# Attention loop with both heads in 64-row tiles of TensorE, walked in half-pair periods

## Chip, cores and metric

One core of a Trainium2 chip runs the whole program, and the metric is the time of the core on the device, in microseconds (us). TensorE has two granted clock levels, 1.2 and 2.4 GHz; the profile writes them as 0.5 and 1.0 of full speed.

## Reference, cut to what matters

Two layers run one after the other on x of 2 x 512 tokens x 128 channels. The first is a FiLM-conditioned transformer block with one head. The second has attention with 16 heads of 64 channels and then an expert-choice mixture with 8 experts. The change is nearly all in the second layer's attention:

```python
qkv = (h @ Wqkv.T).reshape(b, n, 3, H, HD)             # H = 16, HD = 64, b = 2, n = 512
q = _ln(qkv[:, :, 0].transpose(0, 2, 1, 3), qn_g, qn_b)
k = _ln(qkv[:, :, 1].transpose(0, 2, 1, 3), kn_g, kn_b)
v = qkv[:, :, 2].transpose(0, 2, 1, 3)
scores = jnp.einsum('bhnd,bhmd->bhnm', q, k) / jnp.sqrt(jnp.float32(HD))
attn = jax.nn.softmax(scores, axis=-1)
o = jnp.einsum('bhnm,bhmd->bhnd', attn, v)
x = x + o.transpose(0, 2, 1, 3).reshape(b, n, H * HD) @ Wout.T
```

After it come the gate (`softmax(tok @ Wgate.T)`), a top-128 choice of tokens per expert, two expert layers, and the sum into the tokens.

## The kernel before, in words

Each engine has a program of its own, written out by hand, and semaphores order them. The code sets the order on every engine, and nothing else does. PSUM is used as eight banks: `pair0` (banks 0 and 1), `bank[2]` to `bank[5]`, and `pair` (banks 6 and 7).

A pair is two heads of one batch element: 8 head pairs x 2 batch elements are 16 pairs. A unit is one head of a pair with all its 512 queries, so there are 32 units of 4 chunks of 128 queries. The loop runs over units, 8 in one `body`. The first and the last body are written out, and the two between them are turns of a hardware loop whose semaphore waits compare with registers.

For one chunk of one head the engines do this:
- PE: `scores` are two matmuls of 128 rows x 512 columns in the rounded float type F32R (L1304, L1305). The 128 rows hold the head's 64 channels twice, as a high and a low part, in `q_s`, `k_s` and `lows`.
- DVE: the negated row maximum (`negmax`, L894).
- ACT: the exponential with its row sum (`probs`, L602).
- PE, two chunks later: four 128x128 transposes (`turn_probs`, recorded at the helper's line L1113) into `bank[2]` or `bank[3]`.
- ACT (three chunks of four, L608) or DVE (the fourth, L900): the copy of that bank to `probs_T`.

Once per pair, PE multiplies `v_s` with `probs_T` (`mix`, L1328). The two heads take two halves of the output partitions, each a tile of 128 rows x 64 columns of the array. The result is scaled by the transposed reciprocals of the row sums (`turn_recip`, `rec_T`, `o_T`) and goes through `project_out` (L1337) into `x_att`. Once per unit a "piece" of 256 tokens of one pair is prepared: `project` (six F32R matmuls of 384 columns, L1287), a square on ACT (L584) and its sum on DVE, the inverse root on POOL (L431), `qk_n` on DVE, `turn_piece` on PE, an affine step on ACT (L594), and the split into high and low parts on DVE (three casts) and POOL (`lows`, `q_s`: L439, L441).

After the loop ACT computes means, squares and norms of the tokens of batch element 0 and then of 1 (`token_means`, `token_squares`, `token_norm`). In between PE computes the logits (L1434), and ACT does the gate's exponential (L679). Ten `digit` rounds on DVE and PE find the thresholds (`at_least` L1014, counts L1461); in their gaps PE transposes expert weights (`turn_experts`). Then the one-hot matrices are built (L1071 on DVE, L485 on POOL) and the experts run.

## Time and profile before

| what | value |
|---|---|
| median of 3 runs | 438.54 us (437.68 to 440.07) |
| the profiled execution | 440.68 us |
| its span, first to last instruction | 438.9 us |
| mean granted TensorE clock | 0.941 |
| busy: PE, DVE, ACT, POOL | 385.8, 297.2, 272.5, 192.8 us |

The rows below are of that one execution. PE is TensorE's matmuls and PEld its weight loads, which overlap them. The duration of a matmul reaches to the modelled arrival of its last result, so matmuls that follow each other overlap in the record; the distance from start to start is what PE time they take. One matmul of plain 32-bit floats stands in the records as two instructions, one F32R matmul or one transpose as one.

### The profile page before, as it was taken

What the parts mean: (1) busy time and instruction counts of PE and PEld (TensorE: products, weight loads), DVE (VectorE), ACT (ScalarE), POOL (GpSimd) and SP (SyncE); (2) the same over time, 40 slices, a digit from 0 to 9 for tenths busy, and PEclk for the clock granted to TensorE, in tenths of its full rate; (3) what the DMA queues carried; (4) which work ended last, traced back from release to release, by engine and by line L of the source; (5) the groups of instructions that cost most, each with busy time, mean ns of one, the idle gap of its engine ahead of it and who ended that gap; (6) DMA issues with size and microseconds to landing.
All of it is one profiled execution on the core that took longest, in us unless ns stands there. A gap on an engine that the chain in (4) does not pass through costs nothing. (4 is left out here: it accounts for less than half of the span.)

```text
span 438.9 us, 7443 instructions
## 1 busy us (share of the span) xinstructions
PE 385.8 (88%) x2334; PEld 281.2 (64%) x2334; DVE 297.2 (68%) x683; ACT 272.5 (62%) x635; POOL 192.8 (44%) x165
## 2 busy tenths in 40 slices
PE   1899895457999999999999999999999977659996
PEld 1568564345767667677677677677676656448794
DVE  2375557547787787888888878878877537982333
ACT  2145842228777777877877877777778577416441
POOL 5200653646475565564664564664663022063000
PEclk9999996659999999999999999999999995859999
DMA  8400000390000000000000000000000000000001
GB/s 226 135 1 0 3 0 0 99 330 3 2 0 3 0 1 0 3 0 1 2 0 0 0 0 0 0 1 1 0 3 0 1 2 1 1 0 1 1 1 48
DMA packets 7500, 9.58 MB, mean 22 GB/s; under 512 B 371, under 2 KB 4270, under 8 KB 7470
## 3 DMA queue, kind: packets, MB, share of 16 engines
q1 hardware_dynamic: 5646, 7.11, 5.3%
q10 hardware_dynamic: 1824, 2.10, 1.6%
q8 instruction: 16, 0.26, 0.3%
q14 instruction: 14, 0.11, 0.1%
HBM read 8.68 MB, written 0.52 MB: 21 GB/s over the span
## 5 line engine op out<-in xcount | busy, mean ns | idle before, releaser
L894 DVE TENSOR_REDUCE negmax<-pair 128x1 f32<-128x512 f32 x128 | 87.9, 687 | 27.7 <-PE pair L1305 27.2
L602 ACT ACTIVATE probs<-pair,negmax 128x512 f32<-128x512 f32 x128 | 88.1, 688 | 26.4 <-PE bank L1113 17.0
L431 POOL TENSOR_TENSOR qk_rstd<-qk_ms,minus_half 128x8 f32<-128x8 f32 x32 | 52.9, 1653 | 66.2 <-DVE qk_ms L865 66.0
L1113 PE MATMUL bank<-ident,probs 128*128 128x128 f32 x512 | 76.7, 272 | 0.3 <-ACT probs L602 0.3
L608 ACT ACTIVATE probs_T<-bank 128x512 f32<-128x512 f32 x96 | 57.1, 595 | 27.6 <-PE bank L1113 27.6
L1113 PEld LDWEIGHTS bank<-ident,probs 128*128 128x128 f32 x512 | 62.6, 140 | 13.5 <-ACT probs L602 0.5
L1304 PE MATMUL pair<-k_s,q_s 128*128 128x512 f32 x128 | 61.5, 480 | 3.3 <-ACT probs L602 1.9
L1328 PE MATMUL bank<-probs_T,v_s 128*64 128x512 f32 x240 | 58.1, 605 | 0.0
L1305 PE MATMUL pair<-lows,q_s 128*128 128x512 f32 x128 | 50.6, 395 | 0.0
L1304 PEld LDWEIGHTS pair<-k_s,q_s 128*128 128x128 f32 x128 | 24.3, 190 | 35.3 <-issue 17.0
L439 POOL TENSOR_TENSOR lows<-kq,k_s 64x512 fp32r<-64x512 f32 x32 | 41.5, 1296 | 10.4 <-DVE k_s L880 5.8
L441 POOL TENSOR_TENSOR q_s<-kq,k_s 64x512 fp32r<-64x512 f32 x32 | 40.9, 1278 | 1.9
L447 POOL TENSOR_TENSOR rec_wide<-o_rec,ones 128x512 f32<-128x512 f32 x16 | 16.6, 1039 | 46.3 <-DVE o_rec L908 46.3
L1287 PE MATMUL pair<-w_hi,h_hi 128*128 128x384 f32 (+1 forms) x64 | 26.0, 406 | 10.0 <-DVE qk_n L872 7.3
L584 ACT ACTIVATE qk_sq<-pair 128x512 f32<-128x512 f32 x32 | 19.1, 598 | 17.0 <-PE pair L1287 17.0
L594 ACT ACTIVATE kq<-bank,cols 128x512 f32<-128x512 f32 x32 | 24.7, 770 | 7.4 <-POOL q_s L441 5.1
L1328 PEld LDWEIGHTS bank<-probs_T,v_s 128*64 128x64 f32 x240 | 14.5, 136 | 22.2 <-issue 22.2
L900 DVE COPY probs_T<-bank 128x512 f32<-128x512 f32 x32 | 22.1, 689 | 6.9 <-PE bank L1113 6.8
L889 DVE CAST k_s<-k_s 64x512 fp32r<-64x512 f32 x32 | 13.5, 421 | 18.4 <-POOL q_s L441 18.4
L602 ACT ACTIVATION_READ_ACCUMULATOR probs<-pair,negmax 128x1 f32 x128 | 25.4, 198 | 0.0
L1113 PE MATMUL bank<-ident,qk_n 128*128 128x128 f32 x128 | 20.9, 288 | 4.5 <-DVE qk_n L872 4.3
L1305 PEld LDWEIGHTS pair<-lows,q_s 128*128 128x128 f32 x128 | 24.6, 192 | 0.0
(273 smaller groups left out, 738.4 us busy)
## 6 DMA issues: line engine op xcount, KB each, us to landing
fc_raw<-in_L_cond_fc2s_dram SPq DMA_DIRECT2D x1, 2048.0 KB, 15.2
x_in<-in_x_dram ACTq DMA_DIRECT2D x1, 512.0 KB, 4.3
w<-in_L_cond_mlp_w_dram SPq DMA_DIRECT2D x2, 256.0 KB, 3.7
wout<-in_L_cond_Wout_dram SPq DMA_DIRECT2D x1, 512.0 KB
b_all<-in_L_cond_b2s_dram SPq DMA_DIRECT2D x1, 512.0 KB, 11.7
out_dram<-final SPq DMA_DIRECT2D x2, 256.0 KB, 2.4
film<-in_L_cond_film_w_dram SPq DMA_DIRECT2D x2, 128.0 KB, 5.6
wq<-in_L_cond_q_w_dram SPq DMA_DIRECT2D x1, 64.0 KB, 7.7
```

The lines of the kernel that those rows point to most:

```text
L431: pool.tensor_tensor(qk_rstd[:, :, :].rearrange("p c t -> p (c t)"), qk_ms[:, :, :].rearrange("p c t -> p (c t)"), minus_half[:, 0:8], ALU ...
L439: pool.tensor_tensor(piece_at(lows, p_in, 0, HD), kq32[0:HD, :, :], piece_at(k_s, p_in, 0, HD).bitcast(F32), ALU.subtract)
L441: pool.tensor_tensor(piece_at(q_s, p_in, HD, P), kq32[HD:P, :, :], piece_at(k_s, p_in, HD, P).bitcast(F32), ALU.subtract).then_inc(lows_do ...
L594: act.activation(kq32[:, :, :].rearrange("p h n -> p (h n)"), bank[5][:, :], ACT.Identity, bias=col("kq_b"), scale=col("kq_g")).then_inc(k ...
L602: act.activation(probs[:, c % 2, :], bank[c % 2][:, :], ACT.Exp, bias=negmax[:, c:c + 1], accum_out=row_sum[:, j // 2 % 2, j % 2, c:c + 1] ...
L608: act.activation(probs_T[j // 2 % 2][:, j % 2, :, c * P:c * P + P], bank[2 + c % 2][:, :].rearrange("p (k n) -> p k n", k=NC), ACT.Copy).t ...
L894: dve.tensor_reduce(negmax[:, s:s + 1], bank[s % 2][:, :], AX, ALU.max, negate=True)\
L1113: last = pe.transpose(dst[:, n * P:n * P + P], s, ident[:, :])
L1287: last = pe.matmul(in_banks(p)[:, c, 0:W2], h_part[:, at:at + P], w_part[:, bass.ds(group, 1), :].rearrange("p g w -> p (g w)"), start=(n ...
L1304: pe.matmul(bank[c % 2][:, :], q_s[:, slot, h, at], k_s[:, slot, h, :], start=True, stop=False)
L1305: pe.matmul(bank[c % 2][:, :], q_s[:, slot, h, at], lows[:, slot, h, :], start=False, stop=True).then_inc(scores_done, 1)
L1328: last = pe.matmul(bank[4][h * HD:h * HD + HD, :], v_s[:, m % 4, k, h * HD:h * HD + HD], probs_T[m % 2][:, h, k, :], start=(k == 0), stop= ...
```

## The change

The loop is now 32 half-pair periods, all written out; a half is 256 queries of a pair, and a period has two steps of 128 queries of both heads. Its parts:
- **Scores.** `keys_T` and `queries_T` hold one head in partitions 0 to 63 and the other in 64 to 127. A step's `scores` are two plain 32-bit matmuls with 64 rows each, one per half of the array's rows, into two banks. The casts, the high and low parts and their subtractions are gone.
- **Transposes.** `turn_probs` of a step is 16 transposes of 64 partitions, alternating between the two halves of the rows and between `bank[4]` and `bank[6]`. ACT copies the first bank, DVE the second.
- **Order.** The scores of step t are issued a period before its transposes, and `mix` of half r - 1 follows the transposes of half r.
- **Preparation.** ACT copies a projected piece out of PSUM (`qk_raw`); from piece 4 on POOL does the square and `qk_n`. ACT does two affine steps of 256 columns.
- **Before the loop.** `make_weights` also uses 64-partition transposes. Half of `w_lo` moves from POOL to DVE before the loop, the other half to POOL in the first four periods; the load of the expert weights waits for it. Pieces 0 to 3 alternate between `pair` and `pair0`.
- **After the loop.** ACT's token work for batch element 0 moves into the periods 18 to 28. The gate's exponential now stands ahead of ACT's squares of element 1. One `turn_experts` per digit round instead of two, the last four behind the rounds. All one-hot chunks are built on DVE, one 1024-column instruction each.

```diff
-            def scores(g, u, c, j):
-
-                if c == 0:
-                    wait(pe, split_done, u + 2 - j % 2)
-                wait(pe, exp_done, g - 1)
-                at, slot, h = slice(c * P, c * P + P), j // 2 % 2, j % 2
-                pe.matmul(bank[c % 2][:, :], q_s[:, slot, h, at], k_s[:, slot, h, :], start=True, stop=False)
-                pe.matmul(bank[c % 2][:, :], q_s[:, slot, h, at], lows[:, slot, h, :],
-                          start=False, stop=True).then_inc(scores_done, 1)
...
+            def scores(t):
+
+                i, c = t // 4, t % 4
+                wait(pe, exp_done, 2 * t - 2)
                 if c == 0:
+                    pe.wait_ge(kq_affine, 2 * i + 2)
+                for h in range(2):
+                    rows = slice(h * HD, h * HD + HD)
+                    pe.matmul(bank[2 * (t % 2) + h][:, :], queries_T[rows, i % 2, c * P:c * P + P],
+                              keys_T[rows, i % 2, :], start=True, stop=True).then_inc(scores_done, 1)
+
+            def turn_probs(t):
+
+                r = t // 2
+                pe.wait_ge(exp_done, 2 * t + 2)
+                wait(pe, copied_act, t)
+                wait(pe, copied_dve, t)
+                if t % 2 == 0:
+                    pe.wait_ge(kq_affine, min(r + 3, HALVES))
+                    pe.wait_ge(v_placed, min(r + 5, HALVES))
+                    wait(pe, recT_copied, r)
+                for n in range(2 * NC):
+                    for q in range(2):
+                        rows = slice(q * HD, q * HD + HD)
+                        last = pe.transpose(bank[(4, 6)[q]][:, n * HD:n * HD + HD],
+                                            probs[rows, t % 2, n // NC, n % NC * P:n % NC * P + P],
+                                            ident[rows, rows])
...
+            for r in range(HALVES):
+                if 2 * r + 2 < STEPS:
+                    scores(2 * r + 2)
+                turn_probs(2 * r)
+                if 2 * r + 3 < STEPS:
+                    scores(2 * r + 3)
+                turn_probs(2 * r + 1)
+                if r:
+                    mix(r - 1)
+                if r + 3 < HALVES:
+                    turn_piece(r + 3)
+                turn_recip(r)
+                if r + 5 < HALVES:
+                    project(r + 5)
+                if r == HALVES - 1:
+                    pe.wait_ge(copied_act, STEPS)
+                    turn_tokens(0)
+                if r:
+                    project_out(r - 1)
```

The first place is PE's program inside the loop. Before, it ran like this in one unit, from a chunk's scores ahead of a half of `mix` to the next unit's piece:

```order
L1304 MATMUL pair0<-k_s_117,q_s_116 128x512 [waits exp_done]
L1305 MATMUL pair0<-lows_118,q_s_116 128x512
L1113 MATMUL bank3<-ident_49,probs_120 128x128 [waits copied_act,exp_done]
L1113 MATMUL bank3<-ident_49,probs_120 128x128 x3
L1328 MATMUL bank4<-probs_T0_126,v_s_114 64x512 x4
...
L1337 MATMUL bank5<-wout_T_61,o_T_125 128x128 [waits oT_scaled,kq_affine]
L1337 MATMUL bank5<-wout_T_61,o_T_125 128x128 x3
L1287 MATMUL pair<-w_hi_107,h_hi_71 128x384 [waits v_placed,normed]
...
```

Now one period reads like this, from its second `scores` (L1269) on; `bank4` and `pair` alternate in the transposes (L1285):

```order
L1269 MATMUL bank3<-keys_T_116,queries_T_117 128x512
L1285 MATMUL bank4<-ident_49,probs_119 128x64 [waits copied_dve,copied_act,exp_done]
L1285 MATMUL pair<-ident_49,probs_119 128x64
...
L1318 MATMUL bank5<-probs_T_125,v_s_115 64x256 [waits v_placed,out_added,copied_dve,copied_act]
L1318 MATMUL bank5<-probs_T_125,v_s_115 64x256 x7
L1070 MATMUL bank4<-ident_49,qk_n_114 128x128 [waits copied_act,normed]
L1070 MATMUL bank4<-ident_49,qk_n_114 128x128 x3
L1305 MATMUL pair<-ident_49,rec_wide_122 128x128 [waits copied_dve,rec_spread]
...
L1247 MATMUL pair<-w_hi_107,h_hi_71 128x384 [waits h_split,w_split,v_placed]
...
L1296 MATMUL bank5<-wout_T_61,o_T_124 128x128 [waits oT_scaled]
```

The long parts (`mix`, `turn_piece`, `turn_recip`, `project`) now stand together behind both groups of transposes, and each group of transposes waits for the copies of the group before it.

The second place is ACT's program, where before a copy and an exponential alternated and the piece's square stood among them. One period now is this:

```order
L598 ACTIVATE probs_T_125<-bank4 128x8x64 [waits pv_done,probsT_done]
L589 ACTIVATE probs_119,row_sum_120<-pair0,negmax_118 128x512 [waits max_done,probsT_done,o_rec_done]
L589 ACTIVATE probs_119,row_sum_120<-pair0,negmax_118 128x512 [waits max_done,probsT_done]
L598 ACTIVATE probs_T_125<-bank4 128x8x64 [waits pv_done,probsT_done]
L589 ACTIVATE probs_119,row_sum_120<-bank2,negmax_118 128x512 [waits max_done,probsT_done]
L589 ACTIVATE probs_119,row_sum_120<-bank3,negmax_118 128x512 [waits max_done,probsT_done]
L579 ACTIVATE keys_T_116<-bank4,cols_57 128x256 [waits scores_done,kqT_done]
L581 ACTIVATE queries_T_117<-bank4,cols_57 128x256
L562 ACTIVATE qk_raw_109<-pair 128x512 [waits normed,qkv_done]
L566 ACTIVATE v_s_115<-pair 128x256 [waits pv_done]
L605 ACTIVATE rec_T_123<-pair 128x256 [waits oT_scaled,recT_done]
```

The raw copy, the values and the reciprocals come last in the period, and the next period's first transposes wait for them, because `pair` is one of their two banks.

## Rows read from the trace of the kernel before

**Rows 1.** Stretches: us from-to, length, busy PE, PEld, DVE, ACT, POOL, PEclk, DMA share, GB/s.
```profile
82.00:110.00 28.00, 17.54 (x77) 13.88 (x78) 16.01 (x32) 14.15 (x32) 15.69 (x11) 0.73 0.52 169
110.00:346.00 236.00, 234.79 (x1389) 163.03 (x1387) 187.79 (x356) 180.43 (x419) 131.52 (x98) 1.00 0.00 1
```

**Rows 2.** Timeline of PE: scores that open pair 3 and pair 15.
```profile
125.71 0.46 PE L1304 MATMUL pair<-k_s,q_s 128*128 128x512 f32 x1
...
320.22 0.47 PE L1304 MATMUL pair<-k_s,q_s 128*128 128x512 f32 x1
```

**Rows 3.** Timeline of PE and PEld inside a unit: start, us, engine, line, operation.
```profile
200.94 1.94 PE L1328 MATMUL bank<-probs_T,v_s 128*64 128x512 f32 x8
201.43 0.14 PEld L1328 LDWEIGHTS bank<-probs_T,v_s 128*64 128x64 f32 x2 [0.28 <-issue]
201.85 0.14 PEld L1328 LDWEIGHTS bank<-probs_T,v_s 128*64 128x64 f32 x2 [0.28 <-issue]
202.81 0.50 PE L1304 MATMUL pair<-k_s,q_s 128*128 128x512 f32 x1
...
203.38 0.60 PE L1113 MATMUL bank<-ident,probs 128*128 128x128 f32 x4
...
204.72 1.06 PE L1337 MATMUL bank<-wout_T,o_T 128*128 x8
205.53 0.42 PE L1287 MATMUL pair<-w_hi,h_hi 128*128 x1
...
206.70 0.49 PE L1304 MATMUL pair<-k_s,q_s 128*128 128x512 f32 x1
```

**Rows 4.** Chain of waits near the loop's end: start, us, what.
```profile
343.70 0.44 PE bank L1113 x4
...
350.28 1.88 PE bank L1408 x16
```

**Rows 5.** Short transposes: 128 columns loaded, 8 streamed; timeline, and durations (min/median/max ns).
```profile
420.82 0.41 PE L1524 MATMUL pair<-ident,w_rows 8*128 8x8 f32 x4
...
L1524 PE MATMUL pair<-ident,w_rows x4: 202/202/223, 420.8 to 421.0; 8*128 8x8 f32 x4
```

**Rows 6.** Timeline of the short count matmuls with bf16 operands.
```profile
375.68 0.58 PE L1461 MATMUL pair<-at_least,ones_bf 128*128 128x56 bf16 x8 [0.37 <-DVE at_least L1014]
```

**Rows 7.** Groups by line and form: count | busy, mean ns | idle before.
```profile
L602 ACT ACTIVATE probs<-pair,negmax 128x512 f32<-128x512 f32 x128 | 88.1, 688 | 26.4 <-PE bank L1113 17.0 <-DVE negmax L894 6.0
...
L608 ACT ACTIVATE probs_T<-bank 128x512 f32<-128x512 f32 x96 | 57.1, 595 | 27.6 <-PE bank L1113 27.6
L431 POOL TENSOR_TENSOR qk_rstd<-qk_ms,minus_half 128x8 f32<-128x8 f32 x32 | 52.9, 1653 | 66.2 <-DVE qk_ms L865 66.0 <-POOL q_s L441 0.2
...
L900 DVE COPY probs_T<-bank 128x512 f32<-128x512 f32 x32 | 22.1, 689 | 6.9 <-PE bank L1113 6.8
...
L588 ACT ACTIVATE v_s<-pair 128x256 f32<-128x256 f32 x32 | 12.3, 385 | 0.0
```

**Rows 8.** Timeline ahead of the loop.
```profile
66.20 2.61 POOL L419 TENSOR_TENSOR w_lo<-w_all,w_hi 128x1152 fp32r<-128x1152 f32 x1
66.26 3.10 DVE L727 TENSOR_TENSOR xn<-xn,rstd 128x512 f32<-128x512 f32 x1 [1.19 <-POOL rstd L394]
...
76.48 0.68 DVE L727 TENSOR_TENSOR xn<-xn,rstd 128x512 f32<-128x512 f32 x1
...
92.88 0.69 PE L1287 MATMUL pair<-w_hi,h_hi 128*128 128x384 f32 x1 [7.05 <-DVE qk_n L872]
...
94.97 0.63 PE L1304 MATMUL pair<-k_s,q_s 128*128 128x512 f32 x1
```

**Rows 9.** Timeline behind the loop: logits, and DVE behind the gate's exponential.
```profile
358.43 0.28 PE L1434 MATMUL pair<-wgate_T,xa_T 128*128 128x8 f32 x1 [0.78 <-DVE xa_T L990]
...
361.79 0.22 DVE L998 TENSOR_REDUCE gate_m<-gate_x 128x8 f32<-128x64 f32 x1 [1.78 <-ACT gate_x L679]
```

**Rows 10.** Chain of waits inside the digit rounds: start, us, what.
```profile
370.25 1.77 PE bank L1113 x8
```

More of the change, by code:

```diff
@@ L461, in _, with piece_norm @@
-            piece_scale(0, 0)
-            piece_scale(1, 0)
-            piece_low(0, 0, 2)
-            piece_low(1, 1, 2)
-            piece_scale(2, 2)
-            body(0, first=True)
-            with pool.Fori(1, STEPS - 1) as n:
-                body(n)
-            body(STEPS - 1, last=True)
-            spread_recip(PAIRS - 1)
-            for b in range(B):
+            def piece_norm(p):
+                pool.wait_ge(rstd_done, p + 1)
+                wait(pool, kqT_done, p - 1)
+                pool.tensor_tensor(qk_n[:, p % 2, :, :, :], qk_raw[:, p % 2, :, :, :],
+                                   spread(qk_rstd[:, :, :], [P, 2, 4, HD]), ALU.mult).then_inc(normed, 1)
@@ L637, in _ @@
-            piece_in(0, 0, 0)
-            piece_in(1, 1, 0)
-            piece_affine(0)
-            piece_affine(1)
-            piece_in(2, 2, 0)
-            body(0, first=True)
-            with act.Fori(1, STEPS - 1) as n:
-                body(n)
-            body(STEPS - 1, last=True)
+                m, half = p // 2, p % 2 * 2 * P
+                act.wait_ge(kqT_done, p + 1)
+                wait(act, scores_done, 8 * m - 8)
+                act.activation(keys_T[:, m % 2, half:half + 2 * P], turned(p)[:, 0:2 * P], ACT.Identity,
+                               bias=col("keys_b"), scale=col("keys_g"))
@@ new lines, in piece_affine, with exponential @@
+                act.activation(queries_T[:, m % 2, half:half + 2 * P], turned(p)[:, 2 * P:4 * P], ACT.Identity,
+                               bias=col("queries_b"), scale=col("queries_g")).then_inc(kq_affine, 1)
+            def exponential(t, h):
+                if t % 2 == 0 and h == 0:
+                    wait(act, o_rec_done, t // 2 - 1)
+                wait(act, probsT_done, 2 * t - 2)
+                act.wait_ge(max_done, 2 * t + h + 1)
+                act.activation(probs[:, t % 2, h, :], bank[2 * (t % 2) + h][:, :], ACT.Exp,
+                               bias=negmax[:, t % 2, h:h + 1],
+                               accum_out=row_sum[:, t // 2 % 2, h, t % 2:t % 2 + 1]).then_inc(exp_done, 1)
@@ L1274, in _, with project @@
             pe.wait_ge(h_split, 1)
-            pe.wait_ge(w_split, 3)
             pe.wait_ge(wT_copied, W_BANKS + 1)
-            def project(p, p_in, group):
-                if not (isinstance(p, int) and p == 1):
-                    wait(pe, normed, p)
-                    wait(pe, v_placed, p)
+            def project(p):
+                b, g, half = place(p)
+                wait(pe, v_placed, {1: 0, 2: 1, 3: 2}.get(p, p))
+                pe.wait_ge(w_split, weights_ready(g))
+                pe.wait_ge(h_split, b + 1)
@@ L1333, in project_out, with turn_piece @@
-            def project_out(i, group):
-                wait(pe, oT_scaled, i + 1)
-                for c in range(NC):
-                    last = pe.matmul(bank[5][:, c * D:c * D + D], o_T[:, c * P:c * P + P],
-                                     wout_T[:, bass.ds(group, 1), :].rearrange("p g d -> p (g d)"),
+            def turn_piece(p):
+                pe.wait_ge(normed, p + 1)
+                if p >= 3:
+                    pe.wait_ge(copied_act, 2 * (p - 3) + 2)
+                elif p == 2:
+                    pe.wait_ge(kq_affine, 1)
+                turn4(turned(p), [qk_n[:, p % 2, c, 2 * t:2 * t + 2, :].rearrange("p h d -> p (h d)")
+                                  for t in range(2) for c in range(2)]).then_inc(kqT_done, 1)
```

685 lines of the change are left out of this document (291 added, 394 removed).

## The prediction

> **What bounds the kernel now.** I read the stretches first, then the timeline of PE, then the groups. Between 110 and 346 us PE is busy for 234.79 of 236.00 us at a granted clock of 1.00, which is the 2.4 GHz level, while DVE has 187.79, ACT 180.43 and POOL 131.52 [rows 1]. So in the loop the order and the length of PE's work set the time, and what the others need counts only where PE has to wait for it. A pair's first scores lie at 125.71 and, twelve pairs later, at 320.22 [rows 2]. That is 194.51 / 12 = 16.21 us for a pair, or 8.1 us for a half-pair. The durations of matmuls include their way through the array, so I price PE work from start to start.
>
> **What PE does in a half-pair, before and after.** All prices are at the 2.4 GHz level.
>
> - Scores. Before, a chunk of one head costs 203.38 - 202.81 = 0.57 us behind a `mix` [rows 3], and a little less elsewhere. Eight chunks of a pair are four for a half-pair: about 2.2 us. After, a step has two plain 32-bit matmuls of 512 columns, that is four instructions, and a half-pair has two steps. No row has two tiles stacked by rows. The nearest row has two tiles side by side: `mix`, eight instructions of 512 columns in 202.81 - 200.94 = 1.87 us with the change of tiles at both ends [rows 3]. The same work with 256 columns takes 1.88 us for sixteen instructions [rows 4]. The weight loads of two tiles come together and 0.42 us apart from the next two [rows 3]: an instruction of 512 columns costs 0.43 us, and two tiles share it. With two row tiles the same way a step costs 2 x 0.43 = 0.86 us, and a half-pair 1.72. The other end is that the tiles do not overlap: 4 x 0.43 = 1.72 us a step, 3.44 a half-pair.
> - Transposes. Before, four of 128x128 take 0.44 us in the chain [rows 4], and a half-pair has 16: 1.76 us. After there are 32 of half the height, each with 128 columns loaded and 64 streamed. The nearest row is four transposes of 8 rows with the same load and 8 streamed columns: (0.41 - 0.20) / 3 = 0.07 us from one to the next, where 0.20 is the last one's own duration [rows 5]. If the two row tiles don't overlap in their loads, a step costs 16 x 0.07 = 1.12 us. If they do, 8 x 0.07 = 0.56. In between lies the rate at which short instructions come: eight count matmuls with their loads take 0.58 us, and less about 0.2 for the last one's way that is 0.05 each, and 16 x 0.05 = 0.80 [rows 6]. I take 0.87, which is near that row and leaves a little for the wider stream; a half-pair is then 1.74, as before.
> - `mix` of a half has exactly the form of the half-width one at the loop's end, 1.88 us with both changes of tiles [rows 4], the same as half of a pair's 2 x 1.87 now [rows 3].
> - `turn_piece` 0.44, `turn_recip` half of that, 0.22, `project` 206.70 - 205.53 = 1.17 and `project_out` half of 205.53 - 204.72 = 0.81 and a first load, so 0.45 [rows 3]. These are as before.
> - Back into 64-row tiles once a period: `mix` loses 0.16 us (1.87 less 4 x 0.43) for going in and out, so I add 0.1.
>
> The sum is 1.72 + 1.74 + 1.88 + 0.44 + 0.22 + 1.17 + 0.45 + 0.10 = 7.72 us. PE's own work thus hardly shrinks; the same sum for before (2.2 + 1.76 + 1.87 + 0.44 + 0.22 + 1.17 + 0.45) is 8.1, the measured period. The gain on PE is in the scores alone.
>
> **The waits of a period.** I laid one period out from the start of its first transposes, at 0. They end at 0.87, and their last result arrives at 1.05. ACT copies `bank[4]` in 0.60 and DVE its bank in 0.69 [rows 7], until 1.77; `scores` covers this on PE until 1.73. So the second transposes start at 1.83, 0.1 us late. ACT then has two exponentials (0.69 each, until 3.1), the second copy (3.7), and two exponentials (5.1); DVE has copy and three maxima of 0.69 in between and is never the later one. PE goes on with `mix` at 2.7, `turn_piece` 4.6, `turn_recip` 5.0, `project` 5.3 to 6.4, results at 6.6. ACT does its two affine steps from 5.2 to 6.1, then waits for `project`, copies 512 and 256 columns (0.60 and 0.39, overlapping by 0.1) and the reciprocals (0.39) [rows 7], until about 7.8. PE is through `project_out` at 6.8 and the next `scores` at 7.8. The next transposes wait for ACT's last copy and start at 7.8 to 7.9. PE and ACT therefore finish a period together. POOL's square, `qk_n`, inverse root and spread, priced by 2.61 us for 1152 columns [rows 8] and 1.65 for the inverse root [rows 7], are 1.2 + 1.2 + 1.65 + 0.6 = 4.7 us and fit; `qk_n` is needed only at 4.6. I take 7.9 us a period, against 8.1.
>
> **Ahead of the loop.** POOL's `w_lo` (2.61 us) no longer runs beside DVE's `xn`, which took 3.10 us there and 0.68 us where POOL did no such work [rows 8]. That brings the first `project` forward by 2.4 us. The second thing removed is the wait of 7.05 us for `qk_n`, at 92.88 [rows 8], since the raw copy frees the bank. Laid out with the same durations, projections at the lower clock level taking twice as long (this stretch had a mean of 0.73 [rows 1]), the first `scores` come near 89 instead of 94.97 [rows 8]. The first transposes then need two exponentials, a raw copy and two more affine steps, and start near 94.9.
>
> **Behind the loop.** The 32nd period starts at 94.9 + 31 x 7.9 = 339.8, less what the last periods lack: four without `project` (1.17 each, of which about 1.05 shows) and two without `turn_piece` (0.44), 5.1 us together: 334.7. From there PE has transposes (to 2.7), `mix`, reciprocals, the tokens' transposes, `project_out`, the last `mix`, and a chain of scale, `project_out`, add, transposes and copy before the second logits: 11.6 us, so they start at 346.3 instead of 358.43 [rows 9]. That is 12.1 us less. Before, DVE then sat idle for 1.78 us until the gate's exponential was there, which ACT had queued behind its squares [rows 9]; now it goes first, and all but its own 0.24 us goes, 1.5 us. Two groups of expert transposes stood on the chain for 1.77 us in one digit round [rows 10]; one group instead of two leaves 0.9 of it. For the first one-hot chunk, one instruction instead of eight, I allow 0.5 us, an estimate. The transposes moved behind the rounds lie in DVE's gaps. The sum is 12.1 + 1.5 + 1.4 = 15.0 us. The profiled execution takes 440.68 us with its span of 438.9; the median of the runs is 2.1 us lower. Taken off the median: 438.5 - 15.0 = 423.5 us.
>
> **A rule against the change.** Both forms of `mix` [rows 3, 4] show tiles side by side sharing their time, from the first instruction on. The Trainium skill (TensorE: Matmul & The Clock Gate, Part 3) says that matmuls start and end strictly in program order, even in tiles. The two instructions of one head would then have to start before the other head's first, and of the four only the middle two would overlap: 3 x 0.43 instead of 2 x 0.43. The rows of `mix` do not look like that, eight in 1.87 us being four slots and not five, but in a group of four only it would weigh more; it is rival 3. The Trainium skill (TensorEngine Tiling (Array Packing), Key Properties) says that a change of the tiling mode drains the engine; the sum's 0.1 us is from the trace, and rival 4 prices a dearer one.
>
> **The rivals.**
> 1. Forecast, 0.60: periods of 7.6 to 8.1 us, 415 to 430 us.
> 2. The transposes cost 1.12 us or the handovers to ACT and DVE lose as much (four of them, 0.1 us each): the loop stays at 8.2 us a period and only the ends gain. 7.9 + 0.3 gives 423.5 + 31 x 0.3 = 433 us. 0.14. The other way, transposes at 0.56 us give 7.9 - 0.6 = 7.3 and 405 us: 0.05.
> 3. The second head's scores start only beside the first one's second instruction: 0.43 more per step, 0.86 a period, of which PE's sum carries all: 423.5 + 27 = 450 us, 0.06. If the two row tiles don't overlap at all, 1.72 more: 423.5 + 53 = 477 us, 0.09. This is the one on the other side. Its place is L1269; it decides once the row tiles share less than about 70% of their time, since the 15 us are 0.48 us a period. For it speaks that no row shows row tiles; against it that tiles side by side share everything.
> 4. Each of the three changes of tiles in a period costs 0.3 instead of 0.1 us: 0.6 x 31 = 19, 442 us. 0.06. Here too lies a clock that falls in the loop because half-height work leaves PE less active; before, PE kept 1.00 there [rows 1].
>
> **How the numbers follow.** Faster by over 0.5% (about what a measurement of this kernel tells from no change, here 2.2 us) are 1, 2 and its other way, 0.79, less a little for the 4th's neighbours: 0.77. Rivals 3 and 4 are slower: 0.19, and 0.04 is left for between. The range takes in the forecast, 433 and 442 us and leaves out 450 and 477 above and the 405 below: 408 to 446 us. The likeliest case's own range is 415 to 430.
>
> **What would show it.** Right: starts of L1269 0.43 us apart in pairs, a group of 16 transposes (L1285) in 0.8 to 0.95 us, 7.7 to 8.0 us from one `mix` (L1318) to the next, ACT's reciprocal copy (L605) as the last releaser of a period's first transposes, first scores near 89 us, `xn` in 0.68 us twice, logits near 346. Wrong: four starts of L1269 in single file, weight loads of L1285 0.07 us apart in one file, clock rows of 0.5 inside the loop, or PE idle ahead of L1285 behind DVE or ACT for more than 0.3 us a period.

## The result and the profile after

The changed kernel takes 408.81 us (408.0 to 409.49, 4 runs) against 438.51 us (437.68 to 440.07, 4 runs) before: a ratio of 0.9318, 95% interval 0.9286 to 0.935. That is 29.7 us less, twice the 15.0 us of the prediction. The profiled execution has a span of 407.8 us, where before it was 438.9. Both are the slowest of their executions (409.49 and 440.68 us), and the two spans lie 31.1 us apart.

First the stretches of the changed kernel; the columns are those of [rows 1]:

```profile
82.00:100.00 18.00, 12.25 (x76) 6.97 (x75) 9.10 (x18) 11.60 (x30) 5.89 (x5) 0.81 0.00 0
100.00:320.00 220.00, 218.43 (x2135) 144.92 (x2135) 160.04 (x326) 183.42 (x465) 125.23 (x122) 1.00 0.07 23
```

PE is still the bound inside the loop, 218.43 us of 220 at a granted clock of 1.00, as in [rows 1]. So the gain inside the loop has to be PE time that is no longer there. The timeline of PE shows one period (start, duration, engine, line, operation):

```profile
204.92 1.13 PE L1269 MATMUL pair<-keys_T,queries_T 64*128 64x512 f32 x4
205.88 0.24 PE L1285 MATMUL bank<-ident,probs 64*128 64x64 f32 x1
205.88 0.27 PE L1285 MATMUL pair<-ident,probs 64*128 64x64 f32 x1
205.96 0.22 PE L1285 MATMUL bank<-ident,probs 64*128 64x64 f32 x1
205.99 0.22 PE L1285 MATMUL pair<-ident,probs 64*128 64x64 f32 x1
...
206.40 1.11 PE L1269 MATMUL bank<-keys_T,queries_T 64*128 64x512 f32 x4
207.51 0.24 PE L1285 MATMUL bank<-ident,probs 64*128 64x64 f32 x1
...
208.16 1.95 PE L1318 MATMUL bank<-probs_T,v_s 128*64 128x256 f32 x16
210.03 0.66 PE L1070 MATMUL bank<-ident,qk_n 128*128 128x128 f32 x4
210.53 0.38 PE L1305 MATMUL pair<-ident,rec_wide 128*128 128x128 f32 x2
210.66 0.42 PE L1247 MATMUL pair<-w_hi,h_hi 128*128 128x384 f32 x1
...
211.79 0.61 PE L1296 MATMUL bank<-wout_T,o_T 128*128 128x128 f32 x4
212.33 0.70 PE L1269 MATMUL pair<-keys_T,queries_T 64*128 64x512 f32 x2
```

Read it from start to start. The period is 212.33 - 204.92 = 7.41 us, where a half-pair took 8.1 before [rows 2]. The first group of 16 transposes takes 206.40 - 205.88 = 0.52 us, that is 0.032 us for each: the two row tiles share even the loads. The second scores take 1.11 us until the next group, the first ones 0.96. The difference is a wait, and DVE's timeline shows for what:

```profile
206.08 0.69 DVE L872 TENSOR_REDUCE negmax<-pair 128x1 f32<-128x512 f32 x1 [0.63 <-PE pair L1269]
206.68 0.68 DVE L880 COPY probs_T<-pair 128x512 f32<-128x512 f32 x1
```

DVE's copy of the second bank ends at 207.36, and the transposes that overwrite this bank start at 207.51, 0.15 us later. The period's first transposes stand just as far behind ACT's last copy, which ends at 205.73, while they start at 205.88:

```profile
205.34 0.39 ACT L605 ACTIVATE rec_T<-pair 128x256 f32<-128x256 f32 x1
```

At the ends of the loop these rows answer to [rows 8, 9], from the timelines of PE and DVE:

```profile
65.85 0.69 DVE L723 TENSOR_TENSOR xn<-xn,rstd 128x512 f32<-128x512 f32 x1 [1.49 <-POOL rstd L385]
...
88.05 1.23 PE L1269 MATMUL pair<-keys_T,queries_T 64*128 64x512 f32 x2 [1.11 <-ACT queries_T L581]
...
331.41 1.06 PE L1329 MATMUL pair<-wgate_T,xa_T 128*128 128x8 f32 x8 [0.78 <-DVE xa_T L948]
...
333.31 0.22 DVE L956 TENSOR_REDUCE gate_m<-gate_x 128x8 f32<-128x64 f32 x1 [0.32 <-ACT gate_x L673]
```

The first scores come at 88.05 instead of 94.97 us (6.9 less). Of this, 2.2 us lie ahead of the first `project` (70.51 instead of 72.72 us), a mark that moves by as much between executions, and 4.7 us behind it. From the first scores to the second logits it is 331.41 - 88.05 = 243.36 instead of 358.43 - 94.97 = 263.46 us (20.1 less). From the second logits to the end it is 76.4 instead of 80.5 us (4.1 less). Together that is the 31.1 us between the two spans.

### The profile page after: what moved, and what is told of

Its sections match the earlier page's. It is cut to its first block, busy times and chain, and to the rows that moved or that the text cites. A ratio compares the mean times of both kernels' runs of the same rounds, so it can differ in the third digit from the quotient of the medians.

```text
span 407.8 us, 8743 instructions
## 1 busy us (share of the span) xinstructions
PE 365.3 (90%) x3118; PEld 256.1 (63%) x3118; DVE 258.9 (63%) x596; ACT 268.2 (66%) x655; POOL 154.9 (38%) x159
## 4 chain that ended last, share of the span: by engine, by line
PE 81%; DVE 7%; ACT 5%; DMA 2%; issue 2%; POOL 2%; SPq 0%; DVEq 0%; ACTq 0%
PE bank L1318 15%; PE pair L1269 8%; PE pair L1247 8%; PE bank L1070 8%; PE bank L1269 7%; PE bank L1285 6%; PE pair L1285 4%; PE bank L1296 4%; DMA film<-in_L_cond_film_w_dram 2%; PE bank L1210 2%; PE pair L1219 2%; PE bank L1465 2%; PE pair L1305 2%; PE pair L1070 1%; PE pair L1387 1%
## 5 line engine op out<-in xcount | busy, mean ns | idle before, releaser
L1285 PEld LDWEIGHTS bank<-ident,probs 64*128 64x128 f32 x512 | 36.8, 138 | 46.6 <-issue 46.4
L1318 PE MATMUL bank<-probs_T,v_s 128*64 128x256 f32 x512 | 62.3, 385 | 0.6 <-DVE x_att L903 0.6
L872 DVE TENSOR_REDUCE negmax<-pair 128x1 f32<-128x512 f32 x64 | 43.8, 686 | 25.5 <-PE pair L1269 25.5
L598 ACT ACTIVATE probs_T<-bank 128x512 f32<-128x512 f32 x64 | 38.0, 594 | 24.3 <-PE pair L1285 24.1
L589 ACT ACTIVATE probs<-pair,negmax 128x512 f32<-128x512 f32 x64 | 44.0, 687 | 9.6 <-DVE negmax L872 9.4
L1285 PE MATMUL bank<-ident,probs 64*128 64x64 f32 x512 | 43.4, 225 | 2.2 <-DVE probs_T L880 1.3
L1285 PE MATMUL pair<-ident,probs 64*128 64x64 f32 x512 | 45.1, 228 | 0.0
L880 DVE COPY probs_T<-pair 128x512 f32<-128x512 f32 x64 | 43.7, 682 | 1.2 <-PE pair L1285 1.2
L872 DVE TENSOR_REDUCE negmax<-bank 128x1 f32<-128x512 f32 x64 | 43.6, 683 | 0.0
L589 ACT ACTIVATE probs<-bank,negmax 128x512 f32<-128x512 f32 x64 | 43.6, 694 | 0.0
L1269 PE MATMUL pair<-keys_T,queries_T 64*128 64x512 f32 x128 | 37.1, 656 | 2.0 <-ACT queries_T L581 2.0
L1285 PEld LDWEIGHTS pair<-ident,probs 64*128 64x128 f32 x512 | 36.9, 139 | 0.0
L1269 PE MATMUL bank<-keys_T,queries_T 64*128 64x512 f32 x128 | 36.2, 632 | 0.6 <-ACT probs L589 0.6
L894 DVE TENSOR_TENSOR o_T<-bank,rec_T 128x256 f32<-128x256 f32 x32 | 13.6, 425 | 15.2 <-PE bank L1318 15.2
```

What stands on the lines that cost most here:

```text
L589: act.activation(probs[:, t % 2, h, :], bank[2 * (t % 2) + h][:, :], ACT.Exp, bias=negmax[:, t % 2, h:h + 1], accum_out=row_sum[:, t // 2 ...
L598: act.activation(probs_T[:, r % 2, :, :, at:at + HD], bank[4][:, :].rearrange("p (h k n) -> p h k n", h=2, k=NC), ACT.Copy).then_inc(copie ...
L872: dve.tensor_reduce(negmax[:, t % 2, h:h + 1], bank[2 * (t % 2) + h][:, :], AX, ALU.max, negate=True)\
L880: dve.tensor_copy(probs_T[:, r % 2, :, :, at:at + HD], bank[6][:, :].rearrange("p (h k n) -> p h k n", h=2, k=NC)).then_inc(copied_dve, 1)
L1269: pe.matmul(bank[2 * (t % 2) + h][:, :], queries_T[rows, i % 2, c * P:c * P + P], keys_T[rows, i % 2, :], start=True, stop=True).then_inc( ...
L1285: last = pe.transpose(bank[(4, 6)[q]][:, n * HD:n * HD + HD], probs[rows, t % 2, n // NC, n % NC * P:n % NC * P + P], ident[rows, rows])
```

## The experiments

Every kernel is the changed one with the edit shown; the last two build on an earlier edit, which is named there. Each ratio is to the kernel before. The first `project` lies between 68.3 and 71.0 us in the traces of the kernels that have the same program up to there, so small effects are read between two marks of one trace.

### Full-height transposes

```diff
-                for n in range(2 * NC):
+                for n in range(NC):
                     for q in range(2):
-                        rows = slice(q * HD, q * HD + HD)
-                        last = pe.transpose(bank[(4, 6)[q]][:, n * HD:n * HD + HD],
-                                            probs[rows, t % 2, n // NC, n % NC * P:n % NC * P + P],
-                                            ident[rows, rows])
+                        last = pe.transpose(bank[(4, 6)[q]][:, n * P:n * P + P],
+                                            probs[:, t % 2, q, n * P:n * P + P], ident[:, :])
```

ACT and DVE each copy the bank of one head.

> The changed kernel with one thing put back: a step's transposes are eight of 128x128, one head to each of the two banks, and ACT and DVE copy one head each (as many elements as now). Theory A (the loop's gain is that half-height transposes in two row tiles run beside each other): 8 x 0.109 = 0.87 us a group instead of 0.52, so 0.35 x 2 = 0.7 us a period, less up to 0.1 for changes of tiles that are no longer needed: a period of 8.0 to 8.1 us instead of 7.41, and 409 + 31 x 0.65 = 429 us (425 to 431). Theory B (the gain is the order: scores ahead, mix behind, no waits on PE): the transposes hide nothing else, the period stays within 0.1 us of 7.41 and the time within 3 us of 409. The computation is the reference's.

435.72 us, ratio 0.9942 (0.9915 to 0.9968): nearly the whole gain is gone, and the time lies above the 425 to 431 us expected. PE's timeline:

```profile
207.53 1.13 PE L1269 MATMUL pair<-keys_T,queries_T 64*128 64x512 f32 x4
208.59 0.33 PE L1284 MATMUL bank<-ident,probs 128*128 128x128 f32 x1
208.75 0.27 PE L1284 MATMUL pair<-ident,probs 128*128 128x128 f32 x1
...
209.61 1.13 PE L1269 MATMUL bank<-keys_T,queries_T 64*128 64x512 f32 x4
```

The group takes 209.61 - 208.59 = 1.02 us instead of 0.52, and the scores ahead of it 1.06 instead of 0.96. Eight transposes at 0.109 are 0.87 us; the rest is the way into and out of the other tiling, between scores of 64 rows and transposes of 128. The period is 8.34 us. Theory A holds, and its price was too low by the changes of tiles, which I had counted as a saving.

### One row tile, then the other

```diff
-                for n in range(2 * NC):
-                    for q in range(2):
+                for q in range(2):
+                    for n in range(2 * NC):
```

> The changed kernel with the same 16 half-height transposes of a step, but all eight of one row tile and then all eight of the other. Theory A1 (a short transpose is bound by its own tile's weight load and stream, 0.063 us, and the two tiles must alternate to share): 16 x 0.063 = 1.0 us a group instead of 0.52, a period of 8.3 to 8.4 us, 409 + 31 x 0.9 = 437 us. Theory A2 (a short transpose is bound by the rate at which PE takes instructions, 0.032 us each, whichever tile it goes to): nothing changes on PE, and ACT's copy may start up to 0.25 us earlier; 405 to 410 us. The computation is the reference's.

422.64 us, ratio 0.9667 (0.9615 to 0.9719), between the two theories. PE's timeline at the end of the first group:

```profile
203.34 0.28 PE L1285 MATMUL pair<-ident,probs 64*128 64x64 f32 x2
203.41 0.69 PE L1269 MATMUL bank<-keys_T,queries_T 64*128 64x512 f32 x1
203.46 0.35 PE L1285 MATMUL pair<-ident,probs 64*128 64x64 f32 x3
203.65 0.88 PE L1269 MATMUL bank<-keys_T,queries_T 64*128 64x512 f32 x2
```

Each tile still needs 0.063 us for a transpose, so the sharing is by tile and not by the rate of instructions (A1). But the loss is half of what A1 gave. The next step's scores of the first tile start at 203.41, ahead of the last three transposes of the second tile, which come earlier in the program and start from 203.46 on. The two row tiles thus run apart by some instructions. The Trainium skill (TensorE: Matmul & The Clock Gate, Part 3) says that matmuls start strictly in program order; these rows disagree.

### Scores in the form of before, and both forms

```diff
-                    rows = slice(h * HD, h * HD + HD)
-                    pe.matmul(bank[2 * (t % 2) + h][:, :], queries_T[rows, i % 2, c * P:c * P + P],
-                              keys_T[rows, i % 2, :], start=True, stop=True).then_inc(scores_done, 1)
+                    for n in range(2):
+                        last = pe.matmul(bank[2 * (t % 2) + h][:, :], queries_T[:, i % 2, c * P:c * P + P],
+                                         keys_T[:, i % 2, :], start=(n == 0), stop=(n == 1))
+                    last.then_inc(scores_done, 1)
```

`keys_T` and `queries_T` are F32R here.

> The changed kernel with the scores in the form of before on PE: per head two matmuls in F32R with all 128 rows, the same weights in both, while the casts and subtractions for high and low parts stay away. What it computes: every score is twice the sum of both heads' scores, so the probabilities are not the reference's. Theory A (PE's own time is what counts): a step costs 1.08 to 1.14 us as two chunks did before (0.54 to 0.57 each) instead of 0.95, so 0.3 to 0.4 us a period less the change of tiles; 409 + 31 x 0.3 = 418 us (413 to 421). Theory B (the order): within 3 us of 409.

412.88 us, ratio 0.9404 (0.937 to 0.9439), a period of 7.53 us. The second kernel has this edit and the full-height transposes:

> Both of the two runs before in one: full-height transposes and the scores in the form of before, so that only the order of the changed kernel and its lighter work on ACT, DVE and POOL are left; the probabilities are not the reference's. Theory A: PE's sum is that of before, a period of 8.1 to 8.3 us, and only the 15 us at the ends are left of the gain: 422 to 434 us. Theory B: within 5 us of 409.

428.07 us, ratio 0.9751 (0.9715 to 0.9788), a period of 8.07 us. PE's timeline of the second kernel, a step and the second logits:

```profile
205.30 1.18 PE L1269 MATMUL pair<-keys_T,queries_T 128*128 128x512 f32 x4
206.43 0.30 PE L1285 MATMUL bank<-ident,probs 128*128 128x128 f32 x1
...
207.22 0.27 PE L1285 MATMUL pair<-ident,probs 128*128 128x128 f32 x1
207.25 1.18 PE L1269 MATMUL bank<-keys_T,queries_T 128*128 128x512 f32 x4
...
350.90 1.58 PE L1328 MATMUL pair<-wgate_T,xa_T 128*128 128x8 f32 x8 [0.78 <-DVE xa_T L948]
```

With PE's forms of before, the new order takes 350.90 - 87.94 = 262.96 us from its first scores to its second logits, and the kernel before took 263.46. So the order of the loop alone, with all that was taken off DVE and POOL, is worth 0.5 us. What is left of this kernel's gain lies at the ends. The four kernels also give the parts: from both forms of before (8.07), half-height transposes alone bring 0.54 us a period (7.53), half-height scores alone lose 0.27 (8.34), and both bring 0.66 (7.41). Scores in row tiles pay only where the transposes beside them are in the same tiling, and then they bring 0.12 us (7.53 to 7.41): what the second scores save goes into the wait for DVE's copy, which is not there with the longer scores.

### Scores without a second row tile

```diff
-                    rows = slice(h * HD, h * HD + HD)
+                    rows = slice(0, HD)
```

> The changed kernel with both matmul pairs of a step's scores on the rows 0 to 63, so that they can't share time. What it computes: the second head's scores are those of the first head, so its probabilities are not the reference's. Theory A (a 32-bit matmul of 512 columns takes two slots of 0.43 us, and the two row tiles share all of them): a step costs 4 x 0.43 = 1.7 us or a little more instead of 0.96, 0.8 us twice in a period, a period of 8.9 to 9.0 us and 409 + 31 x 1.5 = 456 us (452 to 462), which is the rival 3 of the prediction without any overlap. Theory B (PE has slack that a longer score takes up, above all the wait of 0.15 us): at least 0.3 us a period less than that, under 448 us.

460.03 us (2 runs), ratio 1.0488 (1.0461 to 1.0515). PE's timeline of one step:

```profile
205.16 1.12 PE L1269 MATMUL pair<-keys_T,queries_T 64*128 64x512 f32 x2
206.12 0.27 PE L1285 MATMUL pair<-ident,probs 64*128 64x64 f32 x1
206.13 0.59 PE L1269 MATMUL pair<-keys_T,queries_T 64*128 64x512 f32 x1
...
206.56 0.59 PE L1269 MATMUL pair<-keys_T,queries_T 64*128 64x512 f32 x1
...
206.98 0.22 PE L1285 MATMUL bank<-ident,probs 64*128 64x64 f32 x1
```

A step's scores take 206.98 - 205.16 = 1.82 us, that is four slots, the first of 0.53 and three of 0.43, against 0.96 in the changed kernel: the two row tiles share their whole time. Without the sharing the change would have been 5% slower than before. The second tile has no scores here, and its first transposes start at 206.12, ahead of the first tile's last scores instruction at 206.56, which stands earlier in the program. This is the tiles' separate order again, by more than with one tile's transposes ahead of the other's.

### The second group's wait

```diff
-                wait(pe, copied_dve, t)
                 if t % 2 == 0:
+                    wait(pe, copied_dve, t)
...
-                        last = pe.transpose(bank[(4, 6)[q]][:, n * HD:n * HD + HD],
+                        last = pe.transpose(bank[(4, 6 + t % 2)[q]][:, n * HD:n * HD + HD],
```

DVE's copy reads `bank[6 + t % 2]`.

> The changed kernel with one resource more: the second row tile's transposes go to bank 6 in even steps and to bank 7 in odd ones, so that a period's second group no longer waits for DVE's copy of the first. In the changed kernel that group starts 1.11 us behind its scores, the first one 0.96. Theory A (PE's sum with its handovers is the period): 0.15 us less a period, so 7.26 us and 409 - 31 x 0.15 = 404 us (403 to 406). Rival: ACT's copy of bank 4, which ends 0.15 us before DVE's, or the maxima behind it gate just as late, and the time stays within 1 us of 409. The computation is the reference's.

402.53 us, ratio 0.9183 (0.9157 to 0.9209), the first of these kernels that is faster than the changed one. PE's timeline:

```profile
201.47 1.11 PE L1270 MATMUL bank<-keys_T,queries_T 64*128 64x512 f32 x4
202.41 0.24 PE L1286 MATMUL bank<-ident,probs 64*128 64x64 f32 x1
...
203.06 1.95 PE L1319 MATMUL bank<-probs_T,v_s 128*64 128x256 f32 x16
```

The second scores now take 202.41 - 201.47 = 0.94 us instead of 1.11, and the period is 7.23 us. From the first scores to the second logits it is 237.6 us instead of 243.4, a little more than the 0.15 us a period that were expected.

The opposite edit puts the second `scores` of a period ahead of both groups, so that nothing covers the copies:

```diff
+                if 2 * r + 3 < STEPS:
+                    scores(2 * r + 3)
                 turn_probs(2 * r)
-                if 2 * r + 3 < STEPS:
-                    scores(2 * r + 3)
                 turn_probs(2 * r + 1)
```

> The changed kernel with the two scores of a period ahead of both groups of transposes instead of between them. If the scores are what hides the copies: the second group waits for the last result of the first (0.2 us), DVE's copy (0.69) and its handover (about 0.1), 1.0 us instead of 0.15 now, so 0.8 us a period and 409 + 25 = 434 us (428 to 438). If the copies are hidden anyway or the wait is taken out of another one of the period: under 415 us. The computation is the reference's.

433.66 us, ratio 0.9871 (0.9839 to 0.9903), a period of 8.20 us. PE's timeline:

```profile
205.95 0.22 PE L1285 MATMUL pair<-ident,probs 64*128 64x64 f32 x1
207.08 0.24 PE L1285 MATMUL bank<-ident,probs 64*128 64x64 f32 x1 [0.90 <-DVE probs_T L880]
```

The wait of 0.90 us behind DVE's copy is what the scores hide. Of the new order this is the one piece that was found to count for much: 25 us.

### The ends

```diff
-            act.wait_ge(logits_sub, 1)
-            act.activation(gate_x[:, :, :], gate_x[:, :, :], ACT.Exp).then_inc(gate_exp, 1)
             token_squares(range(NC, TC))
+            act.wait_ge(logits_sub, 1)
+            act.activation(gate_x[:, :, :], gate_x[:, :, :], ACT.Exp).then_inc(gate_exp, 1)
```

The first `w_lo` instruction moves from DVE to POOL in the same kernel.

> The changed kernel with two parts put back outside the loop, which the trace shows apart: ACT's four squares of the tokens stand ahead of the gate's exponential again, and the first half of the low weight parts (w_lo, 1536 columns) is made by POOL beside DVE's xn instead of by DVE earlier. Expected by my theory: the gate's sum on DVE waits 1.5 us longer (1.8 us idle instead of 0.32), xn takes about 3.1 us instead of 0.69, which moves the first project by about 2.4 us, together 409 + 1.5 + 2.4 = 413 us (411 to 415). Rival: xn's 3.10 us before was not POOL's doing but that of another engine or of a DMA beside it; then xn stays at 0.69 us and the time at 409 to 411 us. The computation is the reference's.

412.28 us, ratio 0.94 (0.938 to 0.942). Timelines of DVE and POOL:

```profile
64.29 3.42 POOL L409 TENSOR_TENSOR w_lo<-w_all,w_hi 128x1536 fp32r<-128x1536 f32 x1
```
```profile
64.35 3.91 DVE L725 TENSOR_TENSOR xn<-xn,rstd 128x512 f32<-128x512 f32 x1 [1.49 <-POOL rstd L385]
...
335.75 0.22 DVE L955 TENSOR_REDUCE gate_m<-gate_x 128x8 f32<-128x64 f32 x1 [0.32 <-ACT gate_x L676]
```

DVE's `xn` lasts until POOL's `w_lo` beside it has ended (67.71 us) and then 0.55 us more, nearly its own time: 3.91 us instead of 0.69. From the cast of `w_hi` ahead of it to the first `project` it is 16.7 us, where it is 14.8 in the changed kernel and 14.0 to 15.4 in the others with this part unchanged. So the edit costs 1.3 to 2.7 us there. The Trainium skill (GPSIMD Engine Reference, Specifications) says that VectorE and GpSimd contend for SBUF when VectorE's instruction has two inputs there; the trace agrees. The other half of the expectation failed: the gate's sum waits 0.32 us, not 1.8, though the squares are ahead of the exponential again. They now fit between the last means and the logits. That the time still lies in the expected range is luck.

The next kernel leaves the exponential first, but puts the tokens' work of element 0 behind the loop:

```diff
-                if 0 <= early < NC:
-                    act.wait_ge(out_added, attended(0))
-                    token_means((early,))
-                    token_squares((early,))
...
+            token_means(range(NC))
+            token_squares(range(NC))
+            token_norm(0, range(NC))
+            token_high(0)
```

> The changed kernel with the token work of batch element 0 on ACT and POOL put back behind the loop, while the gate's exponential stays ahead of the squares of element 1. It asks what removed DVE's wait of 1.8 us for the exponential, since moving the exponential back alone did not bring the wait back. My theory now: the tokens' work, which kept ACT busy up to the exponential. ACT then has means, squares, a wait for POOL, norms and a cast of element 0 (about 8 us) behind the loop; the exponential is late by 2 to 4 us, the expert copies too: 411 to 413 us, and a DVE wait on the exponential of 2 us or more. Rival: ACT fits it into its idle time ahead of the logits (3.4 us before the first mean of element 1, 2.4 us before the exponential), and the time stays at 409 us. The computation is the reference's.

410.05 us, ratio 0.9353 (0.9332 to 0.9374). ACT's timeline:

```profile
331.44 0.26 ACT L667 ACTIVATE gate_x<-gate_x 128x64 f32<-128x64 f32 x1 [0.42 <-DVE gate_x L947]
```

ACT is free 0.42 us before the exponential's input is there, so the rival holds. With either of the two edits alone the wait of 1.78 us [rows 9] stays away. In the kernel before, the two stood together; no run puts back both, so that they cause the wait together is argued, not shown.

With two groups of expert transposes in each of the first six rounds:

```diff
-            turn_experts(0)
-            turn_experts(1)
...
-                if n < 2 * E - LATE_TURNS - 2:
-                    turn_experts(n + 2)
+                if n < (2 * E - LATE_TURNS) // 2:
+                    turn_experts(2 * n)
+                    turn_experts(2 * n + 1)
```

> The changed kernel with two groups of expert transposes in each of the first six digit rounds, as before, and none ahead of the rounds or in the last four. Expected: one round is 0.9 us longer than now, since two groups stand between two counts while PE waits for ACT's first copies: 410 us (409 to 411). Rival: the groups lie in gaps of PE, the ten rounds take the 19.3 us of now or less, and the time is the same within 0.5 us. The computation is the reference's.

409.56 us, ratio 0.9319 (0.9286 to 0.9351), the same as the changed kernel. PE's timeline:

```profile
342.14 1.11 PE L1070 MATMUL pair<-ident,fc_raw 128*128 128x128 f32 x4 [1.40 <-ACT fc_T L682]
343.05 1.06 PE L1070 MATMUL bank<-ident,fc_raw 128*128 128x128 f32 x4
343.90 0.58 PE L1385 MATMUL pair<-at_least,ones_bf 128*128 128x56 bf16 x8
```

The wait for ACT's copy and the two groups behind it are there, but nine rounds take 355.16 - 335.34 = 19.8 us against 19.3: 0.5 us, not 0.9.

### Two tries behind the loop

On top of the second bank, ACT copies its first two expert groups before `token_norm`, and three groups instead of two stand ahead of the rounds:

```diff
             token_squares(range(NC, TC))
+            for n in range(2):
+                copy_experts(n)
             token_norm(1, range(NC))
...
-            LATE_TURNS = 4
+            LATE_TURNS = 3
```

> The second bank of the run before, and behind the loop two things more: ACT copies its first two groups of transposed expert weights in its 1.88 us of idle time ahead of token_norm instead of after its table load, and three groups of expert transposes instead of two stand ahead of the first digit round, three instead of four behind the rounds. Expected: the digit round that lasts 2.8 us now (PE waits 1.62 us for ACT's first copy, so that the counts behind it come late) takes 2.0, and the gather starts 0.4 us closer to the first one-hot chunk; 402.5 - 0.8 - 0.4 = 401.3 us (400.5 to 402). Rival: POOL and ACT hand the tokens over later, or the third group ahead of the rounds delays the first count, and nothing is gained against 402.5. The computation is the reference's.

402.71 us, ratio 0.9166 (0.9138 to 0.9194), no different from 402.53, where 400.5 to 402 were expected. PE waits for ACT's copy no more, yet the round still takes 2.8 us. DVE's and POOL's timelines name what I had overlooked:

```profile
333.64 1.26 DVE L988 TENSOR_TENSOR next_base<-next_offset,thr 128x56 int32<-128x56 int32 x1
```
```profile
333.56 1.27 POOL L451 TENSOR_TENSOR tn_lo<-tn,tn_hi 128x512 fp32r<-128x512 f32 x1 [2.42 <-ACT tn_hi L628]
```

An instruction of 0.22 us ends only when POOL's does. The last kernel is this one, with `tn_lo` taken from POOL and given to DVE, into an idle time behind the rounds:

```diff
             token_scale(1)
-            token_low(1)
...
             dve.wait_ge(taken_ready, 1)
+            dve.wait_ge(tn_high, 2)
+            dve.wait_ge(tn_split, 1)
+            dve.tensor_tensor(tn_lo[:, NC:TC, :], tn[:, NC:TC, :], tn_hi[:, NC:TC, :].bitcast(F32), ALU.subtract)\
+               .then_inc(tn_split, 1)
```

> The kernel of z1_second_bank_early_copies with the low part of the second batch element's tokens (tn_lo, 512 columns) made by DVE, in its idle time of 0.60 us between the mask of taken tokens and the slots, instead of by POOL during the digit rounds. There one DVE instruction of 128x56 takes 1.26 us instead of 0.22, from POOL's start to POOL's end (1.27 us), and its round 2.79 us instead of about 2.0. Theory (DVE cannot run an SBUF instruction of this kind beside POOL's): all ten rounds take 2.0 us, the nine intervals 18.1 us instead of 18.9, the one-hot comes 0.7 us earlier against the first comparison (23.4 us instead of 24.1), and the time is 0.7 us less than that kernel's, 402 us (400.5 to 402.5). Rival: the round is long since PE's counts come late there, whatever POOL does; then it keeps 2.8 us and the time stays or grows by DVE's 0.7 us. The computation is the reference's.

402.97 us, ratio 0.917 (0.9148 to 0.9192). The mechanism is right: nine rounds take 344.50 - 326.51 = 18.0 us, and the one-hot comes 23.2 us behind the first comparison instead of 24.1. The time can't show it: the six executions of either kernel spread over 3 us or more (400.15 to 403.87 and 400.25 to 403.28 us), and 0.7 us were expected. And part of it is given back: the stretch of 3 us from the first gather matmul on, in the kernel ahead and in this one:

```profile
354.31:357.31 3.00, 3.00 (x15) 2.58 (x16) 3.00 (x3) 1.34 (x3) 0.00 (x0) 0.82 0.00 0
```
```profile
351.08:354.08 3.00, 3.00 (x13) 2.52 (x14) 3.00 (x3) 0.72 (x2) 0.00 (x0) 0.61 0.00 0
```

The granted clock is 0.61 instead of 0.82. In these 3 us PE is busy at both places, but it comes out of the rounds at the 1.2 GHz level, and the rise comes later against the gather. The expert part is 0.6 us longer than the kernel's ahead (47.9 against 47.3 us from the gather on), of the 0.9 us that were gained.

## Why the prediction was right in sign and half in size

The measured 408.81 us lies 0.8 us above the lower end of the stated range (408 to 446 us) and below the likeliest case's own 415 to 430. That the range holds it is luck: it was drawn to leave out the 405 us of the case that came nearly true, and the ends of the kernel came out close to their forecast.

- **PE's work bounds the loop.** Right. PE is busy for 99% at full clock, and with PE's old forms the new order is worth 0.5 us.
- **The step that failed: the price of the transposes.** I took 1.74 us a period, from the rate of short instructions in one tile [rows 5, 6], with bounds of 0.56 and 1.12 a group. That middle price was the failed step: it let the two row tiles share only part of their time. They take 2 x 0.52 = 1.04. The two tiles alternate at 0.032 us each, and each keeps the 0.063 of its own. That is 0.70 us a period, 22 us over 31 periods. This is the case that the prediction gave as rival 2's other way (0.05).
- **Scores.** 1.72 predicted, 0.96 + 0.94 = 1.90 found (the 0.94 with the second bank, where the wait for DVE's copy is gone): the first slot has 0.53 us instead of 0.43 where `project_out` stands ahead. The sharing itself is complete, so rival 3 is out, as is the strict order: both heads' first instructions start together.
- **Changes of tiles.** 0.10 predicted. `project_out` takes 0.54 us ahead of scores in 64 rows and 0.36 ahead of scores in 128, so 0.17; the second group is 0.65 us ahead of `mix`, the first 0.52 ahead of scores, so 0.13. Together 0.30, rival 4 in small. The Trainium skill (TensorEngine Tiling (Array Packing), Key Properties) says that a change of mode drains the engine; the trace agrees, with 0.13 to 0.17 us.
- **The rest of the sum.** `mix` 1.88 as said; `turn_piece` 0.49 for 0.44, `turn_recip` 0.14 for 0.22, `project` 1.13 for 1.17, `project_out` 0.36 for 0.45.
- **Waits.** 0.1 us at the second group predicted, 0.17 found, behind DVE's copy; the layout has this copy end last too, though it then calls DVE never the later one. ACT's last copy (L605) is as close ahead of the next transposes as the layout said: they start 0.15 us behind its end, the distance found behind DVE's copy. But PE's scores end at the same moment, and the parts found add up to the period without a wait there (1.90 + 1.04 + 1.88 + 0.49 + 0.14 + 1.13 + 0.36 + 0.30 + 0.17 = 7.41). Shorter first scores alone would thus probably not help: `project_out` and the first scores take 0.54 + 0.96 = 1.50 us here and 0.36 + 1.13 = 1.49 with the scores in the form of before. Predicted were 7.9. The difference of 0.49 times 31 is 15.2 us, and that is the shortfall: 12.1 us less up to the second logits predicted, 27.0 found.
- **Ahead of the loop.** Right: the first scores at 88.05 (89 predicted), the transposes at 94.1 (94.9), `xn` at 0.69 us because POOL no longer runs beside it. How near 88.05 is to 89 says little, since that mark moves by 2 to 3 us between executions; the 4.7 us from the first `project` on are the firm part.
- **Behind the loop.** 2.9 us predicted, 4.1 found: 1.5 from the second logits to the first count (3.3 us instead of 4.8), 1.0 in nine rounds (19.3 instead of 20.3), 0.2 from the last count to the gather, and 1.4 from the gather to the end (47.3 instead of 48.7). The gate's 1.5 us are there, but not by the step I named alone, since moving the exponential back changes nothing by itself. The rounds gave the 0.9 us, and two groups in a round explain 0.5 of it.
- **A term that the sum lacked: the clock at the gather.** The 1.4 us behind the gather are no gain of the one-hot instructions. These are the first 3 us from the first gather matmul on, before, in the changed kernel and with one tile's transposes ahead of the other's:

```profile
390.14:393.14 3.00, 2.97 (x10) 2.50 (x11) 3.00 (x16) 0.03 (x1) 3.00 (x6) 0.50 0.00 0
```
```profile
360.49:363.49 3.00, 3.00 (x17) 2.58 (x16) 3.00 (x4) 1.59 (x4) 0.00 (x0) 0.82 0.00 0
```
```profile
373.80:376.80 3.00, 3.00 (x20) 2.56 (x19) 3.00 (x4) 1.89 (x4) 0.00 (x0) 1.00 0.00 0
```

At a granted clock of 1.00 the part from the gather to the end takes 46.8 us, at 0.82 it takes 47.3, at 0.61 (the last kernel above) 47.9, and at the 0.50 of before 48.7. The first three of these have the same program from the gather on, and the kernel before lies in line with them; from the third expert's gather on it is as fast as the changed one (1.8 us an expert), and the gather of the first two takes 5.5 us where the changed kernel takes 4.1. Before, PE had been idle for 2.55 us ahead of the gather, waiting for the one-hot; in the changed kernel it is busy there with the expert transposes that were moved behind the rounds, and the clock rises 1 us into the gather.

## What to carry to other kernels

Where PE bounds a loop, price half-height work by what each row tile does alone and halve it, if the instructions of the two tiles alternate; put all work in the same tiling together, since one part in another tiling can cost more than it brings. A group that overwrites a PSUM bank needs as much other PE work ahead of it as the copy takes, or a second bank: one free bank was worth 6 us here. A gain within a stretch at the low clock can be given back by a later rise of the clock, and a gain behind it can be the clock's alone, so read the granted clock between marks on both sides.

## What was unexpected in the hardware

- Two row tiles keep their own order, not a common one: scores of one tile started 0.05 us ahead of three transposes that stand earlier in the program for the other tile, and with scores on one tile alone the other tile's transposes started 0.44 us ahead of the last of them.
- Two row tiles halve the time of short transposes too, loads included: 0.032 us from one to the next, 0.063 within a tile.
- A DVE instruction of 0.22 us beside a POOL subtraction took 1.26 us, and one of 0.69 took 3.91. DVE's copies and maxima in the loop read PSUM and keep their 0.68 us, though POOL is busy for more than half of that time.
